# Attention key sums: five additions on two engines, masks ahead of them, and another order at the passage into the last stage

## The reference

```python
q, k, v = split(layernorm(x) @ w_qkv.T + b_qkv)     # 32 query heads, 8 key/value heads, 32 wide
q, k = apply_rope(q), apply_rope(k)
scores = q @ k.T / sqrt(32)                          # per head, 512 x 512
scores = where(causal, scores, -1e20)
attn = softmax(scores)                               # over the keys
x = x + layernorm(attn @ v @ w_o.T + b_o)
# feed forward: a base matrix and the two best of 8 low-rank experts (rank 16)
h = layernorm(x)
gate = softmax(top_k(h @ gate_w.T, 2))
ffn = h @ base_w.T + base_b + 2.0 * sum_e gate_e * (h @ lora_A[e].T @ lora_B[e].T)
x = x + layernorm(ffn)
```

## Time and profile before

| | before |
|---|---|
| median of 3 runs | 1059.68 us (1059.44 to 1059.85) |
| the profiled execution, its own time | 1058.27 us |
| its span in the trace | 1056.2 us |
| mean granted TensorE clock | 0.983 |
| PE busy | 1016.7 us, 96% |
| VectorE busy | 637.2 us, 60% |
| GpSimd busy | 411.7 us, 39% |
| ScalarE busy | 400.6 us, 38% |

### The profile page before, as it was taken

How to read it: one execution, slowest core, us unless ns; L and a number is a source line. 1 busy time by engine, 2 the same in 40 slices (tenths; PEclk the granted TensorE clock), 3 DMA queues, 4 the chain that set the end, 5 groups by cost and what they waited for, 6 DMA issues and landing times.

```text
span 1056.2 us, 17673 instructions
## 1 busy us (share of the span) xinstructions
PE 1016.7 (96%) x6614; PEld 830.0 (79%) x6614; DVE 637.2 (60%) x1882; ACT 400.6 (38%) x682; POOL 411.7 (39%) x461
## 2 busy tenths in 40 slices
PE   4999999999989998999999998999999999999995
PEld 4888888898876665666666567899999999999995
DVE  7454442434438776788878846566666666666654
ACT  7132230210117775777776753222222222222221
POOL 1072452432427775778776651121111111111110
PEclk8999999999999998999999999999999999999999
DMA  9144332227246775656555453222222222222101
GB/s 355 53 162 137 120 120 98 102 100 189 80 153 174 189 203 164 160 145 163 133 131 150 123 177 135 80 83 80 80 81 84 81 87 87 83 82 80 58 20 40
DMA packets 78788, 127.31 MB, mean 121 GB/s; under 512 B 7792, under 2 KB 47088, under 8 KB 75632
## 3 DMA queue, kind: packets, MB, share of 16 engines
q1 hardware_dynamic: 78704, 126.19, 39.4%
HBM read 85.27 MB, written 40.37 MB: 119 GB/s over the span
## 4 chain that ended last, share of the span: by engine, by line
PE 87%; POOL 3%; DVE 3%; DMA 3%; ACT 1%; issue 1%; SPq 1%; POOLq 0%; DVEq 0%; ACTq 0%
PE bank L1252 19%; PE bank L1254 19%; PE bank L1253 19%; PE bank L1325 8%; PE bank L1351 7%; PE bank L1367 7%; PE bank L1390 5%; PE bank L1477 1%; PE bank L1261 1%; DVE ln_st L942 1%; DMA att_scratch<-att 1%; DMA q_t<-shift_l 1%; POOL key_sum L705 1%; POOL turn L667 1%; POOL turn L670 1%
## 5 line engine op out<-in xcount | busy, mean ns | idle before, releaser
L1004 DVE CUSTOM_DVE_ANT_0 bank<-bank,row_mask 128x128 f32<-128x128 f32 (+1 forms) x480 | 219.4, 520 | 62.5 <-PE bank L1325 59.2
L653 POOL TENSOR_TENSOR ln_rs<-ln_ve,minus_half 128x1 f32<-128x1 f32 x64 | 61.7, 964 | 402.7 <-DVE ln_mm L947 402.7
L826 ACT ACTIVATE prob<-bank 128x512 f32<-128x512 f32 x320 | 173.7, 598 | 40.4 <-PE bank L1351 40.3
L1252 PE MATMUL bank<-xt_h,wq_h 128*128 128x512 f32 x320 | 127.5, 398 | 4.5 <-DVE wq_l L967 4.5
L1252 PE MATMUL bank<-wf_h,xt_h 128*128 128x384 f32 (+1 forms) x384 | 129.7, 338 | 1.8 <-DVE z L1162 1.8
L1254 PE MATMUL bank<-wf_l,xt_h 128*128 128x384 f32 (+1 forms) x384 | 130.2, 339 | 0.0
L1253 PE MATMUL bank<-wf_h,xt_l 128*128 128x384 f32 (+1 forms) x384 | 129.6, 338 | 0.0
L1325 PE MATMUL bank<-k_t,q_t 96*128 96x384 f32 (+3 forms) x512 | 125.4, 342 | 2.3 <-DVE row_top L1004 2.3
L1254 PE MATMUL bank<-xt_l,wq_h 128*128 128x512 f32 x320 | 125.5, 392 | 0.0
L1253 PE MATMUL bank<-xt_h,wq_l 128*128 128x512 f32 x320 | 125.4, 392 | 0.0
L694 POOL TENSOR_SCALAR_AFFINE_SELECT prob<-prob 128x512 f32<-128x512 f32 x128 | 83.8, 657 | 83.3 <-ACT prob L826 83.3
(11 more groups left out here) (108 smaller groups left out, 1900.1 us busy)
## 6 DMA issues: line engine op xcount, KB each, us to landing
q_t<-q_scratch SPq DMA_DIRECT2D x32, 512.0 KB, 5.3
q_scratch<-turn_h SPq DMA_DIRECT2D x16, 512.0 KB, 2.7
q_scratch<-turn SPq DMA_DIRECT2D x16, 512.0 KB, 3.0
q_t<-q_scratch SPq DMA_DIRECT2D x32, 256.0 KB, 5.5
att_scratch<-att SPq DMA_DIRECT2D x32, 256.0 KB, 2.8
at_raw<-att_scratch SPq DMA_DIRECT2D x16, 512.0 KB, 3.9
x<-x SPq DMA_DIRECT2D x16, 512.0 KB, 4.3
out<-z SPq DMA_DIRECT2D x15, 512.0 KB, 2.9
```

Source lines behind the costliest of these rows:

```text
L653: nc.gpsimd.tensor_tensor(ln_rs[j][:], ln_ve[j][:], minus_half[:], ALU.pow).then_inc(count, 1)
L826: nc.scalar.activation(prob[n % 2][:, i, :, :].rearrange("p h q -> p (h q)"), bank[3 + (NS * n + i) % 3][:], ACT.Exp, scale=INV_SQRT_HD).t ...
L1004: last = nc.vector.tensor_tensor_reduce(out=row, in0=row, in1=row_mask[:, SEQ - w:SEQ], scale=1.0, scalar=LOWEST, op0=ALU.add, op1=ALU.max ...
L1252: mm(dst, a_h, w_h, start=start, stop=False, skip_group_check=True)
```

## The change

There are four parts. GpSimd makes four additions for a group where it made three, VectorE makes a fifth (sum_last: blocks (0,3) + (1,3)), and all masks but the first two go ahead of the second addition. The diagonal blocks (2,2) and (3,3) are now in the key sums, so the denominators need five blocks in three rounds of matmuls and not seven in four; group 31 keeps its fourth round and has two GpSimd additions. The third part is the order around the last group: GpSimd scales y(0) ahead of its last addition, ScalarE takes split_ffn(3) ahead of copy_sums(31), and VectorE waits for GpSimd's operations before it goes on with split_att(1) and split_ffn(3). The fourth: the load of the attention of tile 2 and of its inverses is issued ahead of the last stores, and scale_att(2) stands behind the statistics of y(1).

```diff
--- before.py
+++ after.py
@@ -50,6 +50,7 @@
 NR = len(ROWS)
 SCORES = [(kc, qb) for kc in range(TT) for qb in range(kc, TT)]
 NS = len(SCORES)
+SUMS = 4
 FIRST = [SCORES.index((kc, kc)) for kc in range(TT)]
 FFN_ORDER = (6, 0, 1, 3, 4, 2, 5, 7)
 SPILL = 256
@@ -321,6 +322,7 @@
         prob_ready = sem("prob_ready")
         prob_masked = sem("prob_masked")
         prob_summed = sem("prob_summed")
+        last_summed = sem("last_summed")
         den_ps = sem("den_ps")
         den_ready = sem("den_ready")
         den_stored = sem("den_stored")
@@ -623,6 +625,8 @@
             sp.wait_ge(den_ps, NG)
             load_ffn(5)
             load_ffn(7)
+            load_att(2)
+            load_inverses(2)
             store_att(NG - 1)
             store_den(NG - 1)
             load_res(1)
@@ -635,7 +639,7 @@
                     sp.dma_start(out[t][:, cols], z[:, cols]).then_inc(out_stored, 16)
 
             for t in range(NT + 1):
-                if t + 2 < NT:
+                if 0 < t < NT - 2:
                     load_att(t + 2)
                     load_inverses(t + 2)
                 if t == 2:
@@ -686,6 +690,11 @@
                 if b == 0:
                     scale1(2 * TT + 1)
 
+            def scale_y(t):
+                pool.wait_ge(y_step, 13 * t + 7)
+                wait(pool, y_norm, 2 * t)
+                scale_and_shift(0, y_scale, 4 * t)
+
             def mask(n, kc):
 
                 i = FIRST[kc]
@@ -697,10 +706,13 @@
             def add_keys(n, i, total, a, b):
 
                 pool.wait_ge(prob_ready, NS * n + b + 1)
-                if i < 2:
+                if i == 0:
                     wait(pool, den_ps, n - 1)
+                elif i == 1:
+                    pool.wait_ge(last_summed, n + 1)
                 else:
-                    pool.wait_ge(prob_summed, 3 * n + 2)
+                    pool.wait_ge(prob_masked, TT * n + i + 1)
+                    pool.wait_ge(prob_summed, SUMS * n + i - 1)
                 first = total if a is None else prob[n % 2][:, a, :, :]
                 nc.gpsimd.tensor_tensor(total, first, prob[n % 2][:, b, :, :], ALU.add).then_inc(prob_summed, 1)
 
@@ -716,17 +728,18 @@
                 mask(n, 0)
                 mask(n, 1)
                 add_keys(n, 0, total[:, 0, :, :], SCORES.index((0, 2)), SCORES.index((1, 2)))
-                add_keys(n, 1, total[:, 1, :, :], SCORES.index((0, 3)), SCORES.index((1, 3)))
                 mask(n, 2)
-                add_keys(n, 2, total[:, 1, :, :], None, SCORES.index((2, 3)))
                 mask(n, 3)
+                if n == NG - 1:
+                    scale_y(0)
+                add_keys(n, 1, total[:, 1, :, :], None, SCORES.index((2, 3)))
+                if n < NG - 1:
+                    add_keys(n, 2, total[:, 0, :, :], None, FIRST[2])
+                    add_keys(n, 3, total[:, 1, :, :], None, FIRST[3])
                 if 1 <= n <= NPIECE:
                     piece_lo(n - 1)
 
-            def scale_y(t):
-                pool.wait_ge(y_step, 13 * t + 7)
-                wait(pool, y_norm, 2 * t)
-                scale_and_shift(0, y_scale, 4 * t)
+            def scale_x1(t):
                 pool.wait_ge(y_step, 13 * t + 13)
                 scale_and_shift(0, y_scale, 4 * t + 2)
 
@@ -734,12 +747,13 @@
                 pool.wait_ge(z_step, 9 * t + 8)
                 scale_and_shift(1, z_scale, 2 * t)
 
-            scale_y(0)
+            scale_x1(0)
             for t in range(NT + 1):
                 if t > 0:
                     scale_z(t - 1)
                 if t + 1 < NT:
                     scale_y(t + 1)
+                    scale_x1(t + 1)
 
         @block.scalar
         def _(act):
@@ -908,8 +922,8 @@
             copy_sums(NG - 2)
             normalise_y(0)
             copy_values(NG - 1)
+            split_ffn(3)
             copy_sums(NG - 1)
-            split_ffn(3)
             split_ffn(4)
             normalise_x1(0)
             split_ffn(5)
@@ -1176,6 +1190,14 @@
                 nc.vector.tensor_tensor(wf_l[c][:], wf_raw[c][:], wf_h[c][:].bitcast(F32), ALU.subtract
                                         ).then_inc(wf_ready, 1)
 
+            def sum_last(n):
+
+                wait(dve, den_ps, n - 1)
+                dve.wait_ge(prob_ready, NS * n + SCORES.index((1, 3)) + 1)
+                p = prob[n % 2]
+                nc.vector.tensor_tensor(key_sum[n % 2][:, 1, :, :], p[:, SCORES.index((0, 3)), :, :],
+                                        p[:, SCORES.index((1, 3)), :, :], ALU.add).then_inc(last_summed, 1)
+
             for n in range(NG):
                 after = n + 2 < NG
 
@@ -1192,7 +1214,9 @@
                 maxima_of(3, 4, 5)
                 if n >= KV and n % KV == 2:
                     invert_sums(n // KV - 1)
-                maxima_of(6, 7, 8, 9, 10)
+                maxima_of(6, 7, 8)
+                sum_last(n)
+                maxima_of(9, 10)
                 if n == NG - 3:
                     scale_att(0)
                 if n == NG - 2:
@@ -1204,9 +1228,11 @@
                     scale_att(1)
                     project_bias(0, 1)
                     y_statistics(0)
+            dve.wait_ge(y_scale, 1)
             split_att(1)
             split_ffn(2)
             residual1(0)
+            dve.wait_ge(y_scale, 3)
             split_ffn(3)
             split_ffn(4)
             project_bias(1, 0)
@@ -1225,11 +1251,13 @@
                     ffn_sum(t - 1)
                 if t > 0 and t + 1 < NT:
                     project_bias(t + 1, 0)
-                if t + 2 < NT:
+                if 0 < t < NT - 2:
                     scale_att(t + 2)
                 if t + 1 < NT:
                     project_bias(t + 1, 1)
                     y_statistics(t + 1)
+                if t == 0:
+                    scale_att(2)
                 if t > 0:
                     residual2(t - 1)
                 if t + 1 < NT:
@@ -1373,7 +1401,7 @@
             def denominators(n):
 
                 pe.wait_ge(prob_masked, TT * n + TT)
-                pe.wait_ge(prob_summed, 3 * n + 3)
+                pe.wait_ge(prob_summed, SUMS * n + (SUMS if n < NG - 1 else 2))
                 if n < NG - 2:
                     pe.wait_ge(att_ready, n + 1)
                 elif n == NG - 2:
@@ -1382,13 +1410,21 @@
                 else:
                     pe.wait_ge(den_ready, n)
                 p, total = prob[n % 2], key_sum[n % 2]
-                for i in range(4):
+                for h in range(REP):
+                    dst = den_bank(n)[HD * h:HD * h + HD, :].rearrange("p (b q) -> p b q", q=P)
+                    mm(dst[:, 0:2, :], ones[:], p[:, 0:2, h, :], start=True, stop=False, skip_group_check=True)
+                for h in range(REP):
+                    dst = den_bank(n)[HD * h:HD * h + HD, :].rearrange("p (b q) -> p b q", q=P)
+                    mm(dst[:, 2:4, :], ones[:], total[:, :, h, :], start=False, stop=False, skip_group_check=True)
+                for h in range(REP):
+                    dst = den_bank(n)[HD * h:HD * h + HD, :].rearrange("p (b q) -> p b q", q=P)
+                    last = mm(dst[:, 1:2, :], ones[:], p[:, FIRST[1]:FIRST[1] + 1, h, :], start=False, stop=True,
+                              skip_group_check=True)
+                if n == NG - 1:
                     for h in range(REP):
-                        what, at, w = ((p[:, 0:2, h, :], 0, 2), (total[:, :, h, :], 2, 2),
-                                       (p[:, FIRST[1]:FIRST[1] + 1, h, :], 1, 1),
-                                       (p[:, FIRST[2]:FIRST[3] + 1:2, h, :], 2, 2))[i]
-                        last = mm(den_bank(n)[HD * h:HD * h + HD, P * at:P * (at + w)].rearrange("p (b q) -> p b q", q=P),
-                                  ones[:], what, start=(i == 0), stop=(i == 3), skip_group_check=True)
+                        dst = den_bank(n)[HD * h:HD * h + HD, :].rearrange("p (b q) -> p b q", q=P)
+                        last = mm(dst[:, 2:4, :], ones[:], p[:, FIRST[2]:FIRST[3] + 1:2, h, :], start=False, stop=True,
+                                  skip_group_check=True)
                 last.then_inc(den_ps, 1)
 
             pe.wait_ge(ident_loaded, 16)
```

## The result

| | before | after |
|---|---|---|
| median | 1059.56 us (1059.04 to 1059.85, 4 runs) | 1051.7 us (1048.03 to 1052.32, 4 runs) |
| ratio to before, 95% interval | | 0.9914 [0.9897, 0.9931] |
| the profiled execution, its own time | 1058.27 us | 1052.32 us |
| its span | 1056.2 us | 1050.6 us |
| mean granted TensorE clock | 0.983 | 0.983 |

The account below looks back on a forecast made before the run. PE was taken to bound the regular step. Terms: -12.5 + 1.2 + 2.5 + 3.1 - 2.2 = -7.9 us, profiled time 1050.4, median 1051.8 us; range 1046 to 1056.5, leaving out 2 in 10.

Parts of the forecast that it names:

- The bound and the period: Regular attention step: PE is busy throughout, so dropping a 0.43 us round cuts 9.41 to 8.98 us, 12.5 us over 29 steps.
- The tie of GpSimd and VectorE: Regular step: VectorE's addition holds the shared SBUF port, delaying GpSimd's chain; 0.05 us in 24 steps, +1.2 us (0 to 10).
- both rivals: Regular step: GpSimd becomes the bound, about 1055 us, chance 0.12; or VectorE does, 1065, chance 0.05 slower, 0.05 near nothing.
- The shifts: Regular steps: shift_l is issued 3.07 us before the next scores instead of 3.5, so late landings cost +2.5 us (1 to 4).
- Step 30: First step without row scores: PE waits 2 to 3 us before group 29's denominators; +3.1 us (-1.2 to +3.7).
- The clock's 1.7 us: Step 30: after PE's wait the granted clock drops to the lower level for a while, losing 1.7 us.
- The passage: Into the last stage: 4.5 us wait before the last denominators plus 1.7 clock replaces 8.0; -2.2 us with the shorter round.
- the tiny ln_nm operation loses its turn: Passage, upper bound +1 us: ln_nm loses its turn to split_att(1), 1.2 us more, and one stall stays.

Follow-up runs that it names:

- the second profile: The changed kernel run once more with no edit, and profiled again: 1052.58 us, ratio 0.9932 to the kernel before.

## Why the prediction was right

The time, 1051.7 against 1051.8, is closer than the terms were, and partly by luck. The forecast was built on the profiled execution (1050.4 for it) and put the median 1.41 us above it; the profiled execution took 1052.32, and the median lies 0.6 below. Point by point:

- **The bound and the period: right.** PE fills the step, and it is 8.97 us (8.98 to 9.05 was forecast). The round is worth 0.44, not 0.43.
- **The tie of GpSimd and VectorE: too dear.** 1.2 us were set aside, and nothing is lost: the regular steps are 8.97. The reason is in the timeline above: VectorE's addition meets a mask, and only 0.2 us of it. The margin was judged well, as the doubled addition (0.85 more per step) and the five on GpSimd (0.59 more) show: both engines stand close to their bound. With 0.3 us between GpSimd's last addition and the denominators, both rivals were a few tenths of a us away.
- **The shifts: right in kind, too small.** "S0 waits for shift_l in ten steps" came as said: PE's weight loads waited 4.1 us in 4 steps before. After, who waited for the tile shift_l (us, times):

```profile
  PEld bank L1379: 9.0, 10
  PE bank L1379: 4.7, 4
```

  In the stretch D(0) to D(28) they took 3.8 us more, not 2.5: what exceeds the regular period is 269.9 - 28 x 9.41 = 6.4 us before and 261.4 - 28 x 8.97 = 10.2 after. Here the stall of step 10 alone is 6.5 before and 5.5 after (by chance: it is 6.7 in the second profile), so the nine other steps cost 4.7 us where the prediction had 2.1. Their weight loads waited 0.33 to 1.54 us each. The margin itself was right: shift_l is issued 3.06 us ahead of S0 (3.07 was forecast). The forecast had taken the landing times of before one by one, and after the change other steps were hit, and harder. That the same transfers lie closer together in the shorter step (DMA share 0.60 against 0.55 in the earlier trace rows) may be the reason; no run shows it.
- **Step 30: mechanism right, price an upper one.** PE waits for the key sum at D(29), 1.95 us, as forecast, because scale_att(0) and the split of its attention take turns with GpSimd's three additions:

```profile
595.68 4.72 POOL L717 TENSOR_TENSOR key_sum<-key_sum,prob 128x512 f32<-128x512 f32 x3
...
599.16 2.32 DVE L1095 TENSOR_TENSOR at_l<-at_raw,at_h 128x1024 fp32r<-128x1024 f32 x1 [1.11 <-ACT at_h L847]
```

  Three additions take 4.72 us where they take 3.77 alone. The clock's 1.7 us did not come in the execution of the comparison and did come, with 1.5, in the second one and in six of the experiments (D(29) to D(30) 19.7 to 19.9 us). In three others, which wait there as well, it didn't (18.3 us). By the second profile the stretch D(28) to D(30) is 1.7 us longer than before, where 2.7 were forecast.
- **The passage: the step that was mis-sized.** Forecast were 4.5 us of waiting before D(31) and 1.7 of clock against 8.0 us of old waits and clock, and with the shorter round -2.2 in that stretch; measured are 5.74 and 2.7, and +0.1 in all. The chain is that of the prediction, with its upper bound ("the tiny ln_nm operation loses its turn"): GpSimd's and VectorE's timelines show it.

```profile
617.55 0.84 DVE L1198 TENSOR_TENSOR key_sum<-prob 128x512 f32<-128x512 f32 x1 [8.38 <-ACT prob L840]
...
624.37 1.23 POOL L659 TENSOR_TENSOR ln_nm<-ln_mm,ln_rs 128x1 f32<-128x1 f32 x1
625.55 2.40 POOL L717 TENSOR_TENSOR key_sum<-key_sum,prob 128x512 f32<-128x512 f32 x1
...
624.32 1.22 DVE L1095 TENSOR_TENSOR at_l<-at_raw,at_h 128x1024 fp32r<-128x1024 f32 x1 [0.66 <-POOL ln_rs L657]
625.47 1.36 DVE L1190 TENSOR_TENSOR wf_l<-wf_raw,wf_h 128x1160 fp32r<-128x1160 f32 x1
```

  VectorE stood idle for 8.38 us before sum_last(31), with the split, scale_att(1) and the bias of y(0) behind it in its queue. Then VectorE's split starts 0.05 us ahead of ln_nm on one element per partition and holds it for 1.2; then split_ffn(2) starts ahead of the last addition, which takes 2.40 for 1.29 of work. The prediction had one of these two turns. The first comes from the change's own order: VectorE waits for y_scale to reach 1, which ln_rs does, the first of GpSimd's two operations, and so lets its split go just when ln_nm begins. Waiting for 2 instead was not tried. Both waits at the transposes are gone, as forecast.
- **What the terms don't hold:** the late start of the attention stage, 2.6 us in that one execution, most of it low clock.

So in the spans -8.2 us against a forecast of -7.9 came from a round worth 0.01 more in each step (0.3 in all), a tie that cost 1.2 less, a step 30 that cost 2.5 less in that execution, shifts that cost 1.3 more and a passage that cost 2.3 more. The middle was hit because the misses cancel. The -8.2 leave out the 2.6 us at the start, which this execution had and the second profile did not.

## What to carry to other kernels

Work taken from a full engine is won only as far as the engines that take it up have room at that very place: count each one's step, and then look for the one group where its neighbours are different, which is the last one here; leaving the last group out of the scheme was worth 4 to 5 us. Two changes that each remove a wait at the same passage should be priced together, since one chain runs through both. And look at the single long steps of a regular stretch first: two bias rows loaded side by side cost 5 to 6 us, more than half of what the whole change gave.

## What the hardware showed unexpectedly

- A GpSimd operation on one element per partition took 1.23 us because a VectorE operation with two SBUF inputs had begun 0.05 us earlier. Behind it the two engines went on in turns: split_ffn(2) on VectorE, the addition on GpSimd (2.40 us), then residual1 on VectorE (2.06 us, from 626.97). The Trainium skill, page SBUF — State Buffer, section "SBUF: two separate sides", has the lock for a whole instruction, and the trace agrees (1.23 us, and 2.40 where one addition alone takes 1.29).
- Behind a wait of 1.95 to 1.98 us the clock fell in some executions (0.62 and 0.52 in the windows of 2 us behind it) and stayed at 1.00 in others, of the same kernel. Behind 5.74 us it was at 0.50 to 0.54 in all four profiles with that wait.
- A small DMA of 8 KB (shift_l) took 1.8 to 7.8 us to land. What else is in flight matters: in the nine profiles with the two bias rows loaded side by side the longest landing was 5.6 to 7.8 us, in the five with them apart 4.0 to 5.1.
